# Four row strips: transposed scores issued together with a later unit's maxima products, and the row of maxima carried by a second copy of the queries

## The reference

```python
x = x + jnp.tanh(g_xattn[0]) * _L0_xattn_ref(_layernorm(x, axis=-1), ctx_512, ctx_512)
# x: 32 batches of 128 x 512; ctx: 32 x 128 x 128
NUM_Q_HEADS = 32
NUM_KV_HEADS = 8
qh = q.reshape(B, S, KV, G, D).transpose(0, 2, 3, 1, 4)     # D = 16, G = 4 query heads per kv head
kh = k.reshape(B, S, KV, D).transpose(0, 2, 1, 3)
scores = jnp.einsum('bkgsd,bktd->bkgst', qh, kh) / scale
weights = jax.nn.softmax(scores, axis=-1)
out = jnp.einsum('bkgst,bktd->bkgsd', weights, vh)
```

## Time and profile before

| | us |
|---|---|
| median of 3 runs | 1440.05 |
| lowest, highest | 1434.08, 1441.21 |
| profiled execution | 1444.12 |
| its span | 1442.2 |
| attention stage in it, about | 15 to 449 |

### The profile page before, as it was taken

One profiled execution on the slowest core, in us unless ns is written; L12 is line 12 of the kernel. 1 busy time (PEld: TensorE's weight loads), 2 busy tenths in 40 slices (PEclk: granted clock), 3 DMA queues, 4 the chain that ended last, 5 costly groups with the idle time before them and its releaser, 6 DMA issues.

```text
span 1442.2 us, 33176 instructions
## 1 busy us (share of the span) xinstructions
PE 1332.6 (92%) x12082; PEld 918.3 (64%) x12082; DVE 932.8 (65%) x1627; ACT 543.3 (38%) x847; POOL 412.3 (29%) x470
## 2 busy tenths in 40 slices
PE   3799989797895789989999999999999999999996
PEld 2444444444442667777777777777777777777773
DVE  4897787979765896855545555545444444446887
ACT  2666666767655432222222222222222222222220
POOL 4565455545443710011111111111111111004454
PEclk9965575859555589999999999999999999999998
DMA  6443333334332751136255363546163631167665
GB/s 241 140 133 113 110 132 131 132 104 137 110 133 99 267 190 60 59 132 205 73 179 191 124 212 102 194 144 222 60 211 124 197 108 59 44 212 234 212 206 188
DMA packets 98794, 213.50 MB, mean 148 GB/s; under 512 B 11824, under 2 KB 12336, under 8 KB 98736
## 3 DMA queue, kind: packets, MB, share of 16 engines
q1 hardware_dynamic: 87536, 176.02, 36.1%
q0 software_dynamic: 11200, 36.71, 8.1%
HBM read 228.26 MB, written 66.06 MB: 204 GB/s over the span
## 4 chain that ended last, share of the span: by engine, by line
PE 82%; DVE 8%; issue 4%; DMA 3%; ACT 2%; POOL 1%; DVEq 0%; SPq 0%; ACTq 0%; POOLq 0%
PE PS L1395 38%; PE PS L1414 19%; PE PS L1268 5%; PE PS L1240 5%; PE PS L1252 3%; PE PS L1383 3%; PE PS L1276 3%; DVE negm L841 2%; PE PS L1222 2%; PE PS L1256 1%; DVE xn L827 1%; DMA xnd<-xhl 1%; DMA negR<-negT 1%; PE PS L1286 1%; DVE st L798 1%
## 5 line engine op out<-in xcount | busy, mean ns | idle before, releaser
L1414 PE MATMUL PS<-wb,ghl 128*128 128x512 f16 x1296 | 291.5, 382 | 5.8 <-issue 3.2
L1395 PE MATMUL PS<-uhl,wb 128*128 128x256 f16 x2592 | 293.5, 273 | 2.1 <-DVE uhl L1090 2.1
L1395 PE MATMUL PS<-xT,wb 128*128 128x256 f16 x2592 | 291.8, 273 | 1.1 <-DVE xT L1080 1.1
L1395 PEld LDWEIGHTS PS<-xT,wb 128*128 128x128 f16 x2592 | 253.5, 98 | 30.6 <-issue 1.2
L1395 PEld LDWEIGHTS PS<-uhl,wb 128*128 128x128 f16 x2592 | 252.2, 98 | 31.5 <-DVE uhl L1090 2.4
L1414 PEld LDWEIGHTS PS<-wb,ghl 128*128 128x128 f16 x1296 | 127.4, 98 | 149.9 <-issue 10.2
L841 DVE TENSOR_REDUCE negm<-PS 128x8 f16<-128x1024 f32 x128 | 156.1, 1220 | 75.2 <-PE PS L1240 65.5
L604 POOL COPY ixr<-idx 128x2 int32 x38 | 7.0, 184 | 604.0 <-PE PS L1383 478.4
L1097 DVE TENSOR_TENSOR g<-sl,u 128x512 f32<-128x512 f32 x108 | 74.7, 691 | 146.9 <-ACT sl L761 146.8
L761 ACT ACTIVATE sl<-PS,bb 128x256 f32<-128x256 f32 x216 | 90.5, 470 | 209.7 <-PE PS L1395 209.7
L752 ACT ACTIVATE u<-PS,bb 128x256 f32<-128x256 f32 x216 | 90.4, 470 | 197.0 <-PE PS L1395 164.0
(11 more groups left out here) (153 smaller groups left out, 1597.3 us busy)
## 6 DMA issues: line engine op xcount, KB each, us to landing
wb<-wsc SPq DMA_DIRECT2D x126, 1024.0 KB
wst<-in_wall SPq DMA_DIRECT2D x32, 768.0 KB, 5.9
wsc<-whl SPq DMA_DIRECT2D x32, 768.0 KB, 4.2
ysl<-yb SPq DMA_DIRECT2D x46, 512.0 KB
bd<-in_bdown SPq DMA_DIRECT2D x42, 256.0 KB
X<-in_x SPq DMA_DIRECT2D x8, 1024.0 KB, 8.5
xnd<-xhl SPq DMA_DIRECT2D x32, 256.0 KB, 3.0
xs<-xnd SPq DMA_DIRECT2D x32, 256.0 KB
```

Of the source, the lines that this page charges most:

```text
L1395: ins = pe.matmul(bank[:, hf, (m % 2) * TT:(m % 2 + 1) * TT], wb[:, par, l, k, w, m * P:(m + 1) * P], rhs(x, k), start=(n == 0), stop=(n = ...
L1414: ins = pe.matmul(PS[2][:, t, :], ghl[:, x, k, t * P:(t + 1) * P], wb[:, par, 2, k, w, :], start=(n == 0), stop=(n == len(TERMS) - 1))
```

## The change

`scores_max` and `scores_T` become one function, `scores`, which waits for what both need and then issues a pass of the transposed scores and two heads of the maxima products in turn. The transposed scores have two passes: in the second, the moving operand is `qB`, a copy of the batch's qT in which row 16 of each strip has been overwritten by the negated maxima, and the weights are the keys' low half with ones in row 16 (two memsets of `kx`). `one16` and `negR` are no longer used there. The copy is a DMA per batch on SP's queue (`queries_again`, 128 partitions of 2 KB), and the first row of maxima of a batch now waits for it. Besides, several steps change places in the `body` of TensorE, VectorE and ScalarE, and `norm1` is taken four batches ahead instead of three.

```diff
+            def queries_again(half, par, quad):
+                b = number(half, par)
+                if isinstance(b, int) and b < 2:
+                    sp.wait_ge(S["qT_ready"], b + 1)
+                else:
+                    sp.wait_ge(S["t_done"], UNITS * (b - 1))
+                sp.dma_start(qB[:, par, :, :, :], qT[:, quad, :, :, :]).then_inc(qB_in[par], 16)
             def neg_rows(half, par, pair):
+                if pair == 0:
+                    sp.wait_ge(qB_in[par], 16 * (half + 1))
+                    sp.nop(nofuse=True)
                 sp.wait_ge(S["negT_ready"], 2 * number(half, par) + pair + 1)
-                sp.dma_start(negR[0::STRIP, par, pair, :, :], negT[:, pair, :]).then_inc(neg_in[pair], 16)
+                sp.dma_start(qB[D::STRIP, par, pair, :, :], negT[:, pair, :]).then_inc(neg_in[pair], 16)
...
                 if nx is not None:
                     neg_rows(*nx[:2], 1)
+                if after is not None:
+                    queries_again(*after)
...
+            for par in range(2):
+                g.memset(kx[:, par, 1, :, 1, 0:1], 1.0).then_inc(S["vone"], 1)
...
                 exps(half, par, 1)
+                if not start:
+                    evac_o(*((half - 1, 1) if par == 0 else (half, 0)), 1)
                 if after is not None:
                     evac_q(*after)
-                if not start:
-                    evac_o(*((half - 1, 1) if par == 0 else (half, 0)), 1)
                 exps(half, par, 2)
+                evac_o(half, par, 0)
+                exps(half, par, 3)
                 weights_hi(half, par)
-                exps(half, par, 3)
-                evac_o(half, par, 0)
...
+            def scores(half, par, quad, u, ahead):
                 b = number(half, par)
                 pe.wait_ge(neg_in[u // 2], 16 * (b + 1))
                 need(pe, S["exp_done"], UNITS * b + u)
+                if ahead is not None:
+                    max_waits(*ahead[:2], ahead[3])
+                for w in range(2):
                     for odd in range(2):
+                        part = strip(u, odd, STRIP)
+                        moving = (qT[part, quad, u // 2, :, :], qB[part, par, u // 2, :, :])[w]
+                        ins = pe.matmul(Tb[:, odd, :], kT[part, quad, w, u // 2, :], moving.rearrange("p m c -> p (m c)"),
+                                        start=w == 0, stop=w == 1)
+                    if w == 1:
+                        ins.then_inc(S["t_done"], 1)
+                    if ahead is not None:
+                        for m in range(2 * w, 2 * w + 2):
+                            ins = max_head(ahead[2], ahead[3], m)
+                if ahead is not None:
+                    ins.then_inc(S["m_done"], 1)
```

More of the change, by code:

```diff
@@ L192, in program @@
         neg_in = [sem(f"neg_in{j}") for j in range(2)]
+        qB_in = [sem(f"qB_in{j}") for j in range(2)]
         x_in = [sem(f"x_in{c}") for c in range(XC)]
@@ L324, in body @@
                 nx = follow(half, par, quad, 1)
+                after = follow(half, par, quad, 2)
                 start = isinstance(half, int) and number(half, par) == 0
@@ L879, in _ @@
             maxes(0, 0, 0)
+            norm1(1, 1)
             chunk1(1)
@@ L907, in body @@
                 if nx is not None:
-                    maxes(*nx[:2], 2)
-                weights64(half, par)
+                    evac_neg(*nx[:2], 0)
+                if not (isinstance(half, int) and number(half, par) < 2):
+                    stats2(half - 1, par)
                 if nx is not None:
                     maxes(*nx[:2], 3)
-                    evac_neg(*nx[:2], 0)
-                if not start:
-                    normalise(*pv, 1)
+                if isinstance(half, int):
+                    v.wait_ge(S["ln1_ready"], chunks_by(number(half, par) + 1))
+                if fourth is not None:
+                    norm1(*fourth[:2])
+                weights64(half, par)
                 if isinstance(half, int) and number(half, par) == 1:
@@ L918, in body @@
                     maxes(*after[:2], 0)
-                if not (isinstance(half, int) and number(half, par) < 2):
-                    stats2(half - 1, par)
+                if not start:
+                    normalise(*pv, 1)
                 if nx is not None:
@@ L1301, in body @@
                 pv = (*((half - 1, 1) if par == 0 else (half, 0)), (quad - 1) % 4)
-                scores_T(half, par, quad, 0)
-                if nx is not None:
-                    scores_max(*nx, 1)
-                if not start:
-                    tr_o(*pv[:2], 0)
+                scores(half, par, quad, 0, nx and (*nx, 1))
                 if after is not None:
                     tr_k(*after[:2])
-                scores_T(half, par, quad, 1)
-                if nx is not None:
-                    scores_max(*nx, 2)
+                if not start:
+                    outputs(*pv, 1)
+                scores(half, par, quad, 1, nx and (*nx, 2))
                 if after is not None:
```

64 lines of the change are left out of this document (28 added, 36 removed).

## The result

| | before | changed |
|---|---|---|
| median, us | 1440.63 (4 runs) | 1377.38 (4 runs) |
| lowest, highest | 1434.08, 1442.82 | 1374.25, 1378.48 |
| profiled execution, us | 1444.12 | 1378.48 |
| its span | 1442.2 | 1376.6 |

The changed kernel takes 0.9565 of the time before (95% interval 0.9529 to 0.96). The forecast was 1403 with a range from 1385 to 1427, so it was wrong: right in sign, but the gain is 63 us where 37 were forecast. What happened is rival (b), the clock share, with more on top.

A forecast was written before the change was run, and what follows sets the result against it. TensorE was taken to bound the attention stage at 1.2 GHz and VectorE at 2.4. Gains of 33 us in the middle, 1 in front and 3 in the tail made 37, hence 1403 us, range 1385 to 1427.

The forecast's parts named there:

- rival (b): Attention stage: clock at the upper level 60% of the time, 10.75 us a batch, 1382 us in all; chance 0.12.
- at the same clock mix: Middle batches: 0.7 x 11.95 + 0.3 x 9.9 = 11.3 us, plus 0.15 for hand-overs, 11.45 a batch.
- (a): Attention stage: the clock stays at the lower level, a gain of only 16 us, 1424 in all; chance 0.17.
- my 33: Gain forecast for the 23 middle batches: from 12.90 to 11.45 us each, 33 us.
- the dropped pass: TensorE's transposed scores: two passes instead of three and one unit put in step, 2.27 us less a batch at 1.2 GHz.
- the moved xn: VectorE: xn no longer blocked by GpSimd's L554 for 1.8 us; work drops from 10.39 to 8.6 us a batch.
- A batch at 2.4 GHz: Middle of the attention stage: four reductions and the gaps between them, 9.9 us a batch against 11.17.
- xn meeting GpSimd's qx subtraction: VectorE at 2.4 GHz: xn may meet this 1.15 us GpSimd step; 0.7 us a batch allowed for it.
- A batch at 1.2 GHz: Middle of the attention stage: the loop of TensorE and VectorE takes 11.95 us a batch against 13.45.
- Front: First 6 batches, 82.04 us: statistics ahead of the third reduction lengthen the loop; gain 0 to 1, taken as 1 us.
- Tail: End of the attention stage: last scores chain loses four passes (1.7 us), outputs' wait goes (about 1); gain 3 us.
- rival (d): The wait for both partners or the copy eats the gain: 1.5 us more a batch, 1435 to 1442; chance 0.06.

The follow-up runs named there:

- before_xn_moved: The kernel before with only VectorE's xn moved from the head of its batch to behind the first negT copy, taken a batch earlier: 1370.84 us.
- the fillers: Runs with unused 128x128 fp16 matmuls added on TensorE, among them ten a batch in the changed kernel (1365.25 us) and six in the kernel before (1425.13 us).
- joint_waits: The kernel before with two passes, xn moved, and each unit's scores also waiting for the reduction that the maxima products need: 1367.84 us.
- three_passes: The changed kernel with the transposed scores in three passes again and no second copy of the queries: 1438.47 us.
- xn_in_hole: The changed kernel with xn moved behind the key copy, where VectorE waits but GpSimd's weights subtraction runs: 1405.67 us.
- stats_in_hole: The changed kernel with VectorE's statistics moved from ahead of the third reduction to behind the key copy: 1356.6 us.
- three_passes_filler: The changed kernel with three score passes, no copy of the queries, and ten idle matmuls a batch added on TensorE: 1383.78 to 1446.12 us.

## Why the prediction was wrong

**The step that failed: "at the same clock mix".** I took the share of before, 30% at 2.4 GHz, and put the other cases into rivals (a) and (b) with 0.29 together. It was 72%. What the old share would have given can be read from the changed kernel's own batches: 9.22 us at clock 1.00 and 11.49 at 0.70 is 0.76 us for each tenth; the batch at 0.84 (10.46) lies on that line. Carried on to 0.65, a batch would be 9.22 + 3.5 x 0.76 = 11.9 us, (12.90 - 11.9) x 23 = 23 us, an estimate. So of the middle's 61 us, about 23 are work and waits saved and about 38 are the clock. Set against the first alone, my 33 was about 10 too high.

**The reasoning behind it.** I read the earlier trace rows as "TensorE is full at 1.2 GHz, so its length is what counts", and asked only what less work on TensorE does to the clock. The rows had more: at 2.4 GHz VectorE held the batch, and TensorE had holes. The 11.17 us that I took for a batch at 2.4 GHz was not quite one either: its clock is 0.87, and no batch of that middle was wholly at 2.4 GHz. The next rows are that batch, a stretch of before wholly at 2.4 GHz, and one of before_xn_moved:

```profile
245.47:256.64 11.17, 9.40 (x128) 4.63 (x126) 10.27 (x15) 8.61 (x12) 6.27 (x5) 0.87 0.43 142
248.50:265.00 16.50, 12.01 (x190) 6.79 (x186) 16.12 (x23) 12.04 (x15) 10.95 (x9) 1.00 0.53 173
```

```profile
162.50:213.00 50.50, 42.33 (x679) 24.58 (x669) 45.17 (x74) 43.91 (x53) 30.32 (x25) 1.00 0.47 157
```

VectorE is busy 16.12 of 16.50 us in the second row, and TensorE 12.01, 0.73 of the time; with VectorE relieved (third row) it is 0.84. So the relief makes TensorE denser at 2.4 GHz, and it stays there for over 50 us at a time, where the middle of before never had more than 17. That it stays is shown (0.65 to 0.89 with its own work unchanged). That density is the reason is not: the fillers speak for it, and joint_waits, which kept 2.4 GHz with 0.73, against it.

**Which part the gain was put down to.** I gave the gain to the dropped pass: 2.27 us a batch at 1.2 GHz. In the old order it is worth 8 to 11 us in all, and the moved xn, which I had as 1.8 us of VectorE's work, 70 to 73. The change as made needs both: without the pass dropped (three_passes) it gains nothing, with xn blocked (xn_in_hole) it loses 28 of 63.

**Terms of the sum.** A batch at 2.4 GHz: 9.9 forecast, 9.22 measured. The 0.7 between them was for xn meeting GpSimd's qx subtraction, and it never did: that ran from 205.21 to 206.37, xn at 207.31. Without it, the 9.2 of the working stood. A batch at 1.2 GHz: 11.95 forecast, not tested, as none ran; 11.49 at 0.70 points to more, by the line above an estimated 13.0. Front: 1 forecast, 2.6 measured. There I had rightly seen that the statistics lengthen the loop, but 1 us a batch was too little: moving them freed 1.9 (11.1 us over 6 batches), part of it perhaps by the clock. Tail: 3 forecast, 8.5 measured, to the last oT transpose (which ended near 453.7 before, 385.1 now). I counted only the scores chain and a wait of the outputs there; the clock, 0.63 to 0.79, and VectorE's shorter work are likely to have given the rest, which was not taken apart. The expert stage took about 3 us more than before (988.5 to 991.5), which I had at nothing; I did not look into it. And rival (d) was added up wrongly: 1.5 us a batch on top of (a)'s 1424 is 1458, while the 1435 to 1442 given there is the same 1.5 us on top of the forecast.

**What held.** The interleaving is worth nothing. The copy costs nothing in the middle. It lands in 2.4 us, against 3.0 in the nearest row. The estimated 2.6 came from a fit that the Trainium skill (DMA: Bandwidth & Descriptors, Anatomy of one DMA) gives for DMAs issued by GpSimd, while SP issues this one; it is close all the same. At the start it is not so clear: TensorE waits 3.14 us for the first row of maxima, which now stands behind the copy, and whether that is the copy was not tried. xn is clear of L574, which starts 2.0 us into the batch where 1.9 was derived. The joint unit takes 0.57 us where 0.47 was laid out (204.91 to 205.48). The new bound is the loop of TensorE and VectorE, with holes ahead of joint units put down to the reduction.

## What to carry to other kernels

Where the granted clock moves between its levels inside the stage that is changed, the share of the two levels is not a constant of the sum but its largest unknown: give the forecast a case for each direction, with real weight. Read a batch at each level separately, and ask of an edit to any engine what it does to TensorE's holes at 2.4 GHz, not only to the engine that looks full at 1.2. And before giving a large gain to the part with the long name, run the smallest moved line alone: here one VectorE operation, moved by some lines, was worth more than the whole change.

## What the runs showed of the hardware

- More TensorE work can be faster: ten idle matmuls a batch took 12 us off the changed kernel and 12 off stats_in_hole, six took 15 off the kernel before. Where the clock was at 0.98 already they took nothing off.
- One program can get different shares of the two levels: the four executions of three_passes_filler spread over 62 us, the slower the lower their mean clock (0.946 to 0.889).
- A TensorE with holes can keep 2.4 GHz: for 69 us on end in joint_waits, busy 50.65 of them.
- A TensorE that is busy 13.04 us of 13.04 at 1.2 GHz is not thereby granted 2.4 GHz (before_xn_moved, 224.38 to 237.42).
- What GpSimd's 3.1 us subtraction blocks depends on the operation: xn, begun 0.16 us behind it, took 3.23 us instead of 0.53; bn_stats, begun 0.60 behind it in stats_in_hole, its usual 0.68.
